# Cross-attention on one core: two score units in one exponential, in the last two batches

## The reference

```
Q = relu(x @ Wq + bq);  K = relu(ctx @ Wk + bk);  V = relu(ctx @ Wv + bv)
attn = softmax(Q_h . K_h / sqrt(8), masked where a key row sums to 0)   # per head, 100 x 1444
attn = attn * (query row does not sum to 0)
out = concat_h(attn @ V_h) + x
```

## Time and profile before

| | |
|---|---|
| median of 3 runs | 360.11 us |
| profiled execution, its own time | 360.41 us |
| its span in the trace | 358.5 us |
| TensorE busy | 349.2 us (97%) |
| ScalarE busy | 300.4 us (84%), of which 384 exponentials 293.3 |
| VectorE busy | 236.6 us (66%) |
| one exponential of 121 x 800 | 841 ns |

### The profile page before, as it was taken

The page is one execution under the profiler, slowest core; times in us unless marked ns, Lnnn a source line. Parts: engine busy times, 40 slices in busy tenths (PEclk is TensorE's granted clock), DMA queues, the critical chain, the costliest instruction groups (busy, mean ns, idle before and its releaser), DMA issues.

```text
span 358.5 us, 16853 instructions
## 1 busy us (share of the span) xinstructions
PE 349.2 (97%) x6706; PEld 243.6 (68%) x6706; DVE 236.6 (66%) x777; ACT 300.4 (84%) x397; POOL 7.2 (2%) x30
## 2 busy tenths in 40 slices
PE   8899899999999999999999999999999999999994
PEld 5657576776767677676767767676776767677662
DVE  5948887593948659394866839486684939579321
ACT  1488588888989888898989889898988888898993
POOL 6010000000000000000000000000000000000000
PEclk9999999999999999999999999999999999999999
DMA  6658748775664638366463837546373754537000
GB/s 205 218 144 306 241 155 322 225 254 177 232 190 158 195 121 286 92 240 181 168 189 130 273 91 257 165 166 206 135 252 91 275 148 168 176 110 236 10 11 5
DMA packets 40398, 64.55 MB, mean 180 GB/s; under 512 B 28084, under 2 KB 29364, under 8 KB 40372
## 3 DMA queue, kind: packets, MB, share of 16 engines
q1 hardware_dynamic: 39442, 63.26, 55.0%
q10 hardware_dynamic: 930, 0.90, 0.7%
HBM read 13.73 MB, written 0.82 MB: 41 GB/s over the span
## 4 chain that ended last, share of the span: by engine, by line
PE 92%; DVE 4%; DMA 1%; ACT 1%; issue 1%; ACTq 1%; DVEq 0%
PE psum L629 36%; PE psum L605 29%; PE psum L551 13%; PE psum L542 12%; DMA wq_sb<-in_Wq 1%; PE psum L703 1%; DVE k_raw L830 1%; ACT k_parts L502 1%; DVE late_low L1075 0%; ACT probs L511 0%; DVE k_high L849 0%; DVE k_cent L849 0%; PE psum L572 0%; DVE query_bd L902 0%; DVE k_low L854 0%
## 5 line engine op out<-in xcount | busy, mean ns | idle before, releaser
L511 ACT ACTIVATE probs<-psum 121x800 f32<-121x800 f32 x384 | 293.3, 841 | 41.1 <-PE psum L605 41.1
L629 PE MATMUL psum<-probs,values 121*32 121x200 f32 x3072 | 153.6, 333 | 0.0
L629 PEld LDWEIGHTS psum<-probs,values 121*32 121x32 f32 x3072 | 96.0, 110 | 42.1 <-issue 18.7
L605 PEld LDWEIGHTS psum<-query_bd,k_parts 64*121 64x121 f32 x1536 | 91.8, 181 | 45.9 <-issue 40.1
L605 PE MATMUL psum<-query_bd,k_parts 64*121 64x200 f32 x1536 | 115.7, 281 | 1.1 <-ACT k_parts L502 0.9
L830 DVE TENSOR_SCALAR_CACHE_REDUCE k_raw<-psum,bk_sb 128x361 f32<-128x361 f32 (+2 forms) x63 | 37.6, 598 | 80.1 <-PE psum L542 80.1
L551 PE MATMUL psum<-wv_sb,keyT 128*32 128x129 f32 (+1 forms) x1536 | 54.7, 277 | 0.0
L542 PE MATMUL psum<-keyT,wk_mixed 128*32 128x361 f32 (+2 forms) x504 | 52.4, 489 | 1.2 <-DVE k_raw L830 1.2
L883 DVE TENSOR_SCALAR values<-v_biased,keep 121x128 f32<-121x128 f32 x192 | 43.2, 283 | 6.3
L551 PEld LDWEIGHTS psum<-wv_sb,keyT 128*32 128x32 f32 (+1 forms) x1536 | 38.1, 108 | 6.7 <-DMA bv_sb<-in_bv 0.4
L873 DVE TENSOR_TENSOR v_biased<-psum,bv_sb 121x384 f32<-121x384 f32 x64 | 35.0, 548 | 0.0
(11 more groups left out here) (81 smaller groups left out, 78.7 us busy)
## 6 DMA issues: line engine op xcount, KB each, us to landing
k_parts<-k_high SPq DMA_DIRECT2D x30, 722.0 KB, 5.0
k_parts<-k_low SPq DMA_DIRECT2D x30, 722.0 KB, 5.5
keyT<-in_ctxT SPq DMA_DIRECT2D x15, 722.0 KB, 4.3
query_rep<-late_high SPq DMA_DIRECT2D x2, 600.0 KB, 7.7
query_rep<-late_low SPq DMA_DIRECT2D x2, 600.0 KB, 7.8
residual<-in_x SPq DMA_DIRECT2D x64, 12.5 KB
k_parts<-k_high SPq DMA_DIRECT2D x2, 480.0 KB, 3.4
k_parts<-k_low SPq DMA_DIRECT2D x2, 480.0 KB, 3.4
```

Of the source, the lines that this page charges most:

```text
L511: nc.scalar.activation(probs[0:KTILE, u % PROB_SLOTS], scores_ps[0:KTILE, u % SCORE_SLOTS, :, 0:QCOLS], ACT.Exp, scale=SCALE).then_inc(pro ...
L605: mm = nc.tensor.matmul(scores_ps[0:KTILE, u % SCORE_SLOTS, j, n * TCOLS:(n + 1) * TCOLS], k_parts[rows, parity, t, kt * KTILE:(kt + 1) * ...
L629: mm = nc.tensor.matmul(spans[c * VCOLS:(c + 1) * VCOLS, half, :, :, 0:SPAN], values[0:KTILE, parity, kt, half * HALF_PAIRS + c, :], probs ...
```

## The change

In batches 14 and 15 ScalarE takes the units a and b of each cycle in one instruction (121 x 1600, four banks) and c in another. It waits for the later of the two units' scores, and for the value products of the later of the two units that used the `probs` slots before; it counts `probs_ready` up by two when the whole instruction is done. The hardware loop covers batches 1 to 12, and batch 13 is written out as batch 15 was. TensorE's and VectorE's programs are the same.

```diff
+            def batch_by_pairs(b):
+                for first in range(0, UNITS, CYCLE):
+                    for u, units in ((first, 2), (first + 2, 1)):
+                        act.wait_ge(scores_ready, UNITS * b + u + units)
+                        act.wait_ge(pv_done, UNITS * b + u + units - PROB_SLOTS)
+                        at, slot = u % PROB_SLOTS, u % SCORE_SLOTS
+                        nc.scalar.activation(probs[0:KTILE, at:at + units], scores_ps[0:KTILE, slot:slot + units, :, 0:QCOLS],
+                                             ACT.Exp, scale=SCALE).then_inc(probs_ready, units)
+
             batch(0, 0)
-            pairs_loop(act, 1, B - 1, batch)
-            batch(B - 1, 1)
+            pairs_loop(act, 1, B - 3, batch)
+            batch(B - 3, 1)
+            batch_by_pairs(B - 2)
+            batch_by_pairs(B - 1)
             store_last(act, 1, range(1, HALF_PAIRS, 2))
```

## The result

The changed kernel takes **362.92 us** (median of 7 runs, 362.71 to 364.54), the kernel before beside it 360.11 (360.0 to 360.51). The ratio is 1.0083, 95% interval 1.0069 to 1.0097: slower by 2.8 us. Forecast was 361.0 in a range of 359.8 to 361.9: the right direction, a third of the size.

The account below looks back on a forecast made before the run. Only the last eleven cycles could react, bound by ScalarE and a loop through both engines. Start + 0.21, ten cycles + 0.77, end - 0.06 make + 0.92 on 360.11: 361.0 us, range 359.8 to 361.9.

Parts of the forecast that it names:

- Batch 13 written out and the shorter loop ... Price 0: ScalarE's code layout: its sequencer work lies in cycles where ScalarE has 0.3 us free a cycle, so no cost.
- About 2.27 us a cycle: Late cycles without side work: pair 1.51, release 0.05, scores and start 0.71, together 2.27 us a cycle.
- both loops: New loop, pair end to next pair, 2.27 us; old loop through ScalarE and TensorE, 4.53 over two cycles; both 2.27 a cycle.
- the hand-over: Between ScalarE and TensorE: a and b released together, next pair waits until both are scored; ScalarE idles 0.16 us a cycle.
- the late start: The pair starts when a and b are scored, 0.71 us after a's scores start, in place of 0.50.
- 0.67 + 0.04 = 0.71: From the start of a's scores to the pair: eight score matmuls 0.67 us, then 0.04 to the start.
- It holds, with only 0.05 to spare: First five cycles of batch 14, with side work: c's exponential releases at 2.99 us, c's scores due at 3.04; price 0.
- The second wait ... Price 0: The pair's wait for value products six units back is covered by the 0.71 us wait for its own scores.
- a and b are released together: Both slots come free at the pair's end; before, a's came free 1.45 us before c's.
- Rival 1: ScalarE's pace decides in the late cycles, which fall to 2.11 us: 359.3 us, chance 0.05.
- Rivals 2 and 3: Pair's length: cheap at 1.34 us gives 359.8 us, chance 0.12; nothing saved by joining, 1.68 us, gives 363.0, chance 0.10.
- Rival 4: TensorE's granted clock falls to half for one cycle: 362.7 us, chance 0.05.

Follow-up runs that it names:

- e2: The changed kernel without pairs: batches 14 and 15 by single exponentials, layout as in the change, 13 to 15 written out; 361.25 us (1.0030).
- e1: The changed kernel with ScalarE's batches 1 to 13 in a loop of one batch a turn, the pairs the same; 361.67 us (1.0042).
- e10: The changed kernel with ScalarE's batches 11, 12 and 13 written out in place of 13 alone; 362.80 us (1.0071).
- e3: As e1, but each pair is two instructions of 121x800: the first waits for both units' scores, the second counts probs_ready by two; 361.70 us (1.0040).
- e6: As e3, but each of the two instructions waits for its own scores, so only the joint release is left; 360.33 us (1.0001).
- e4: As e1, but a pair counts probs_ready up by one, and TensorE waits for the counts that this makes; 361.19 us (1.0045).
- e5: As e3, but each of the two instructions counts probs_ready by itself, so only a's late start is left; 361.42 us (1.0034).

## Why the prediction was wrong

- **The failed step is "Batch 13 written out and the shorter loop ... Price 0".** I priced ScalarE's sequencer work in batch 13 and not the code as such. The written-out code stops ScalarE once, at its 110th instruction after the loop, for 1.3 us, of which 1.1 to 1.25 arrive at the end (e2 - before 1.1, change - e1 1.25, e10 - e1 1.1). The sentence "without that cover it would still be two loop turns less" shows the error: more straight code had no rival and no row. It is also miscounted: a turn is two batches, so it is one turn less. With the pairs alone (e1, 361.67) the time would have been inside the range to 361.9, though above the forecast's own 360.5 to 361.5.
- **"About 2.27 us a cycle": mechanism right, size off.** The pair's length (1505 ns for 1.51), c's start after it (1.40 for 1.39), the release (0.05) and both loops were right; e3 to e6 show that the hand-over is the cause, and in it mainly the late start (1.16 of e3's 1.58). The term mis-sized is "0.67 + 0.04 = 0.71" from a's scores to the pair: it is 0.765, since the pair's wait is an instruction of its own. Ten cycles make about 0.5 us of it, and e4 gets 0.44 back.
- **"It holds, with only 0.05 to spare"** (cycles with side work) failed with that term, once: the third burst of scores for a pair starts 2.67 us after the second, and in the kernel before it is 2.62. The other steps there stayed as they were, and e4, without the separate wait, has 2.63. It is + 0.05 us.
- **"The second wait ... Price 0"** held, though the reading behind it is loose: the value products from 346.55 last 1.22 in the earlier trace rows, to 347.77 and not 347.70. In the changed kernel they are counted 0.97 us or more before each late pair starts, its scores 0.07 before.
- **The order of the costs.** The text puts "a and b are released together" beside the late start. e6 shows the release at nothing by itself, e5 the late start at 1.16. Together (e3, 1.58 over the kernel before) they cost more than the two apart, as the forecast's new loop needs both.
- **Rivals.** Rival 1, ScalarE's pace, is out: the late period grew, and ScalarE idled 0.1 us a cycle in it. Rivals 2 and 3 fall with 1505 ns; rival 3's number, 363.0, is near the result for a wrong reason. Rival 4, the clock, did occur in the profiled execution, but after the stall, and it is not in the median.

The sum, as measured, has two parts. The pairs are + 1.55 (e1): 0.92 as forecast; 0.54 for the separate wait, by the traces of e1 and e4 (0.44 in the ten cycles and 0.10 before them, the held cycle in it); and 0.09 left over, which no run divides further. The place in the code is + 1.25, the change less e1. Together that is 2.80, measured 2.81.

## What to carry to other kernels

Joining two instructions saves only what their starts are apart beyond the work, 0.06 us here. Price first the loop that they close: from the first input's being ready to the joined start, and through every engine back. With three score slots this loop decided here, although ScalarE looked fully busy. When an edit writes out loop bodies, run the layout without the edit: the stall came at a fixed place in the code, and the profile put it down to another engine.

## What the runs showed of the hardware

- ScalarE stalled for 1.3 us at the 110th instruction after the loop in three kernels (the changed one, e2 and e10, with 122, 154 and 218 instructions there), and nowhere where 58 to 106 follow. A packet of instructions starts 0.4 to 0.9 us after the 109th and 1.6 to 1.8 before the 110th. What sets 110, and whether a different layout gets them in time, stays open.
- Counting a semaphore by two moved the wait out of the instruction, which then started 0.05 us later (0.07 after the count in e1, 0.02 in e4).
- TensorE's order matters beyond its sum: value products right after scores 1.15 us, after projections 1.02; scores cut in two 0.99 for 0.81.
